# A quantised convolution and a spectral layer on one core: one row copy moves from VectorE to GpSimd, the per-image copies to ScalarE, and the per-image steps are spread out

## What is computed

```python
# layer 0: group norm, then a 3x3 convolution of int8-valued data, added to x
q  = clip(round(gn(x) * 127 / max|gn(x)|), -127, 127)
qw = clip(round(w * 127 / max|w|), -127, 127)
x  = x + conv3x3(q, qw) * (sx * sw / 127**2) + bias
# layer 1: group norm, then a mixing of 32 x 16 low frequencies, added to x
xf = rfft2(gn(x))[:, :, 32 rows, 16 columns]
x  = x + irfft2(einsum('ijab,ejab->eiab', R, xf))
```

## Time and profile before

| | us |
|---|---|
| median of three runs | 3821.65 |
| the profiled execution | 3827.99 |
| its span in the trace | 3826.2 |
| first stage, up to the first quantised tile | 786 |
| second stage, from the first quantised tile to the last | 786 to 2412 |
| per-image steps of the last image, mixing | 2430 to about 2550 |
| third stage | to the end |

### The profile page before, as it was taken

One profiled execution on the slowest core, in us unless ns is written; L12 is line 12 of the kernel. 1 busy time (PEld: TensorE's weight loads), 2 busy tenths in 40 slices (PEclk: granted clock), 3 DMA queues, 4 the chain that ended last, 5 costly groups with the idle time before them and its releaser, 6 DMA issues.

```text
span 3826.2 us, 82423 instructions
## 1 busy us (share of the span) xinstructions
PE 3155.1 (82%) x33434; PEld 1600.3 (42%) x33529; DVE 3273.9 (86%) x3398; ACT 2359.9 (62%) x3507; POOL 823.1 (22%) x1040
## 2 busy tenths in 40 slices
PE   5555556569999999999999999898888888888886
PEld 1111111146666666666666666673222222222222
DVE  6777888899999999989899999459888888888887
ACT  5777777758888887878788888433333333333332
POOL 0000000035455454545454544200000000000000
PEclk7777776689999999999999999759999999999998
DMA  9999999989999999999999999629999999999998
GB/s 366 358 360 357 360 367 359 343 240 355 336 316 341 309 352 298 354 299 349 302 348 323 327 336 316 198 96 424 427 427 427 427 427 427 427 425 421 421 421 372
DMA packets 342545, 1352.61 MB, mean 354 GB/s; under 512 B 45792, under 2 KB 47040, under 8 KB 243808
## 3 DMA queue, kind: packets, MB, share of 16 engines
q1 hardware_dynamic: 223104, 811.13, 58.9%
q0 software_dynamic: 82272, 268.58, 19.7%
q10 hardware_dynamic: 36864, 268.45, 16.7%
HBM read 811.10 MB, written 536.87 MB: 352 GB/s over the span
## 4 chain that ended last, share of the span: by engine, by line
DMA 41%; DVE 26%; PE 21%; ACT 5%; issue 4%; SPq 1%; POOL 1%; DVEq 0%; ACTq 0%
DMA out<-ring 18%; DMA ring<-in_x 12%; DVE ring L555 9%; DMA ring<-x_scratch 9%; PE ps L713 6%; DVE area L537 4%; ACT area L308 4%; PE ps L724 4%; PE ps L675 4%; DVE area L532 3%; DVE ring L650 2%; DVE area L541 2%; DMA x_scratch<-ring 2%; PE ps L734 2%; PE ps L816 1%
## 5 line engine op out<-in xcount | busy, mean ns | idle before, releaser
L284 POOL DMA_DIRECT2D x_scratch<-ring x1024 | 817.1, 805 | 1606.7 <-DVE ring L555 1583.9
L858 PE MATMUL ps<-x,gj_s 128*128 128x512 bf16 x2977 | 767.7, 407 | 221.2 <-DVE ring L650 213.8
L713 PE MATMUL ps<-area,wq 128*32 128x512 bf16 x12264 | 769.8, 385 | 58.0 <-DVE ring L555 32.8
L650 DVE TENSOR_TENSOR ring<-ps,ring 128x1024 f32<-128x1024 f32 x512 | 603.1, 1219 | 162.1 <-DMA ring<-x_scratch 158.7
L555 DVE SCALAR_TENSOR_TENSOR ring<-ps,sc,ring 128x1024 f32<-128x1024 f32 x512 | 634.6, 1278 | 22.4 <-PE ps L713 15.1
L675 PE MATMUL ps<-ring,negm_s 128*32 128x512 f32 x2048 | 387.4, 897 | 314.8 <-DMA ring<-in_x 314.8
L333 ACT ACTIVATE area<-ps 128x512 f32<-128x512 f32 x1024 | 553.4, 595 | 128.6 <-PE ps L724 127.5
L858 PEld LDWEIGHTS ps<-x,gj_s 128*128 128x128 bf16 x3072 | 295.0, 103 | 772.1 <-DVE ring L650 440.4
L724 PE MATMUL ps<-id_s,ring 128*128 128x128 f32 x4096 | 563.6, 281 | 17.8 <-ACT area L333 13.9
L461 DVE TENSOR_REDUCE stat<-area 128x1 f32<-128x4096 f32 x128 | 559.1, 4409 | 6.0 <-ACT area L308 5.8
L724 PEld LDWEIGHTS ps<-id_s,ring 128*128 128x128 f32 x4096 | 445.1, 142 | 169.3 <-issue 101.9
(11 more groups left out here) (123 smaller groups left out, 2158.9 us busy)
## 6 DMA issues: line engine op xcount, KB each, us to landing
ring<-in_x SPq DMA_DIRECT2D x256, 1024.0 KB, 7.8
ring<-in_x SPq DMA_DIRECT2D x1024, 256.0 KB, 6.7
x_scratch<-ring POOLq DMA_DIRECT2D x1024, 256.0 KB, 6.5
ring<-x_scratch SPq DMA_DIRECT2D x256, 1024.0 KB, 11.7
out<-ring ACTq DMA_DIRECT2D x256, 1024.0 KB, 25.3
ring<-in_rt SPq DMA_DIRECT2D x1, 4096.0 KB, 13.8
area<-in_gj SPq DMA_DIRECT2D x1, 768.0 KB, 4.5
eh_s<-in_eh SPq DMA_DIRECT2D x1, 128.0 KB, 2.1
```

Of the source, the lines that this page charges most:

```text
L284: pool.dma_start(x1_rows[b, m, r], xslot(t % SL)[32 * r:32 * r + 32, :].rearrange("p (g w) -> p g w", g=4)).then_inc(s_x_out[t % SL], 16)
L650: nc.vector.tensor_tensor(half, ps[0][:, hj * 2 * HW:(hj + 1) * 2 * HW], half, ALU.add).then_inc(s_add, 1)
L713: last = mm(ps[0][32 * cg:32 * cg + 32, HW * g:HW * g + HW], wq[:, (3 * a + dw) * C:(3 * a + dw + 1) * C], src[:, 1 + dw:1 + dw + HW], sta ...
L858: last = mm(bank(j), gj_s[:, (j * 3 + v) * 128:(j * 3 + v + 1) * 128], (z12, z12, z13)[v][:, k % 2], start=(v == 0), stop=(v == 2))
```

## The change

VectorE's lower-row copy (`q[64:128]` to `qs[0:64]`) goes to GpSimd, which makes it between its stores, with a semaphore of its own (`s_ql`) that the convolution waits for beside `s_q`. GpSimd's loop now runs over steps: in step i it stores tile i-3, then copies the rows of tile i. The eight `rows_copied` of each image go from VectorE to ScalarE. The later per-image steps are put at other j, and the loops run five steps longer, T + 20. In the diff `...` marks lines left out.

```diff
+        s_ql = sem("quantised_lower_rows_copied")
...
-            for t in range(T):
+            def lower_rows(t):
+                g0 = 4 * (t % 4)
+                pool.wait_ge(s_r, t + 1)
+                nc.gpsimd.tensor_copy(qs[0:64, g0:g0 + 4, :], q[64:128, g0:g0 + 4, :]).then_inc(s_ql, 1)
+
+            def store(t):
                 b, m = divmod(t, TB)
                 pool.wait_ge(s_ev, 2 * t + 2)
...
+            pool.wait_ge(s_qt, 1)
+            for i in range(T + 3):
+                if i >= 3:
+                    store(i - 3)
+                if i < T:
+                    lower_rows(i)
...  (scalar)
+            def rows_copied(b, n):
+                act.wait_ge(s_vt, 8 * b + n + 1)
+                act.activation(vt[:, :, 4 * n:4 * n + 4, :],
+                               bank(7).rearrange("p (c g k) -> p g c k", c=4, g=8), ACT.Copy).then_inc(s_vte, 1)
...
-                if small and j == 5:
+                if small and j == 6:
                     h_copied(b)
+                if small and 1 <= j < 5:
+                    rows_copied(b, 2 * j - 1)
                 if 4 <= i and i - 4 < T:
                     turned(i - 4, 0)
                     turned(i - 4, 1)
                     squared(i - 4)
+                if small and j < 4:
+                    rows_copied(b, 2 * j)
+                if 4 <= i and i - 4 < T:
                     turned(i - 4, 2)
                     turned(i - 4, 3)
-                if small and j == 8:
+                if small and j == 12:
                     root(b)
...  (vector)
-                nc.vector.tensor_copy(qs[0:64, g0:g0 + 4, :], q[64:128, g0:g0 + 4, :])
...
-                if small and 1 <= j < 5:
-                    rows_copied(b, 2 * j - 1)
...
-                if small and j < 4:
-                    rows_copied(b, 2 * j)
-                if small and j == 6:
+                if small and j == 8:
                     sums(b)
-                if small and j == 7:
+                if small and j == 11:
                     variance(b)
-                if small and j == 9:
+                if small and j == 14:
                     spectrum(b)
...  (tensor)
                 if h == 0:
                     pe.wait_ge(s_q, t + 2)
+                    pe.wait_ge(s_ql, t + 1)
...
-                if small and j == 6:
+                if small and j == 7:
                     dc_first(b)
-                if small and j == 7:
+                if small and j == 9:
                     spread(b)
-                if small and j == 9:
+                if small and j == 12:
                     spectra(b)
```

More of the change, by code:

```diff
@@ L361, in _ @@
             scaled(0)
-            for i in range(T + 15):
+            for i in range(T + 20):
                 b, j = divmod(i - (TB + 5), TB)
@@ L556, in combine @@
                                                op0=ALU.mult, op1=ALU.add).then_inc(s_ev, 1)
[L558 to L561, removed]
             def sums(b):
```

## The result

The change makes the kernel slower: 3857.09 us median (four runs, 3853.67 to 3862.18) against 3824.45 us for the kernel before on the same chip (3821.11 to 3829.39), a ratio of 1.0078 with a 95% interval of 1.006 to 1.0097. Run again beside the experiments it gave 1.0075 (1.0049 to 1.01). The prediction was 3765 us and faster.

What follows compares the result with a forecast made beforehand. VectorE was taken as the bound at 5.92 us a step, TensorE next at 5.75. From 3828.0 us, 55 for the images and 2 for the first 37 steps gave 3771 profiled, 3765 us median; range 3745 to 3835.

Steps and rivals of the forecast that it cites:

- What bounds the kernel: Second stage, plain steps: VectorE sets the pace at 5.92 us a step, TensorE's own pace is 5.75 us.
- VectorE's part: One copy of 0.72 us with its gap leaves each step, 5.92 to 5.20 us; waits of 5.0 us an image go.
- GpSimd's part: The new copy between stores takes 1.9 us and has 2.3 us of room under L555; GpSimd works 5.3 us a step.
- The rival on the other side: GpSimd's copy is slow and blocks VectorE; from about 2.7 us a net loss, about 3920 us at 3.5; chance 0.20.
- TensorE's part: As the next bound, TensorE takes 198.4 us an image instead of 206.5, a gain of 55 us over 6.81 images.
- ScalarE's part: The eight row copies an image moved to ScalarE cost nothing, 6.4 us a step against TensorE's 6.85.
- the late loads: ScalarE's waits for loads in the second stage: an allowance of 1.3 us an image.
- the time after the last tile: The per-image chain behind the last tile changes by zero, between -1 and +1 us.

Runs made afterwards that it cites:

- Experiment 1: The changed kernel with GpSimd's copy waiting for VectorE's last row copy of the tile instead of its rounding; 3804.69 us against 3831.47, ratio 0.9928.
- experiment 9: The changed kernel with GpSimd's copy replaced by a memset of the same 64x2064 elements at the same place; 4272.68 us in a single run.
- experiment 5: Kernel of Experiment 1 with the short per-image VectorE operations taking their second operand as a scalar from memory; 3786.14 us against 3826.52, ratio 0.9891.

## Why the prediction was wrong

- **What bounds the kernel** was right: VectorE at 5.92 us a step, TensorE behind it at 5.75. Experiment 1 puts plain steps at 5.76. A slip of the working, 37 x 0.19 where 5.92 - 5.75 gives 0.17, changes nothing, since 2 us were taken.
- **VectorE's part** was right in what it took away, 177 us of row copies and 44 us of `mixb` copies over the whole run, and wrong in that nothing came back. What came back is 174 us in the long pieces, 12 us in held scalings and 15 us in the root's multiplication. Its sum used the plain step of the earlier trace rows for all tiles. The tile in four with two pieces was in it as a few hundredths of a microsecond; it is the tile that decided.
- **GpSimd's part** is the step that failed. The copy's length was forecast as 1.9 us and measured as 1.92, its start 3.4 us behind the combining and measured as 1791.52 - 1788.15 = 3.4. The error was the sentence that it has "2.3 us of room, all of it under L555": I took the port as held from the copy's start to its end. For this copy it is taken once the copy has been let go and VectorE leaves it free, 0.96 us ahead of the start here, with two stores still ahead of the copy in GpSimd's order. In the tile with a seam between two copies that costs 2.7 us, 64 times. Of the two-input operations of the per-image work, which the prediction did not list among those that can be held, one an image is held in the changed kernel and two in experiment 1, for 2.2 us each.
- **The Trainium skill** (SBUF — State Buffer, "Who interferes with whom") says that a VectorE operation with two SBUF inputs contends with a GpSimd operation that reads SBUF and not with one that only writes. The runs agree on the copy, 2.37 us instead of 0.16 beside it. On a memset no run here shows it, since in experiment 9 these operations never ran beside one. I had weighed this section against L555 alone, where it says no and the trace says no (1.28 us after as before), and had not gone through the short operations with it.
- **The rival on the other side** named the right mechanism and the wrong condition: it asked for a copy of 2.7 us or more. A copy of 1.92 us was enough, through its early release. No term and no rival gave the release a price, and the result lies 22 us above the range.
- **TensorE's part** (198.4 us an image) was optimistic by about 2 us: with the holds of pieces and two-input operations gone, experiment 5 has images of 197 to 203, mean 200.5. The gain that the prediction put at 57 us is 40 us there.
- **ScalarE's part, the late loads and the time after the last tile** came out as said: ScalarE waits less for loads than before (49.6 us against 85.5), the added wait of TensorE on GpSimd's copy never shows, and the rest of the program behind the last tile is 1413 us against 1414.

## What to carry to other kernels

When a copy goes from VectorE to GpSimd, look at what VectorE does from the moment that the copy's wait is satisfied, not from the moment it would run: every seam between two of VectorE's fast copies and every operation with two SBUF inputs in that time can be held until GpSimd's operation ends. Let GpSimd's operation wait for the last of VectorE's operations that share the port, even if its data are ready earlier: here that moved one wait by 0.8 us and was worth about 1.5%. And cost a lighter engine on its rarest step too: a step that comes once in four or once in 32 has its own order and can undo the gain of the others.

## What the runs showed of the hardware

- A GpSimd copy of 64x2064 bf16 elements takes 1.92 us, a memset of them 1.84, a copy of 64x516 0.62 and of 64x4 0.20.
- A 64x1548 copy on VectorE takes 3.26 us instead of 0.55, and an operation on 128x1 elements with two SBUF inputs 2.37 instead of 0.16, when GpSimd's copy of 1.92 us has been let go ahead of them. The wait begins up to 0.96 us ahead of the copy's start in the trace.
- VectorE's scaling of 128x1024 float32 elements takes up to 2.28 us instead of 0.80 when GpSimd's copy is already running beside it.
- A GpSimd memset holds VectorE's copy behind the rounding that released it, 1.15 us ahead of its own start: 3.55 us instead of 0.69 for 64x2064 elements.
- GpSimd's descriptor work for four stores takes 3.31 us beside VectorE's copies, 2.89 beside a held one, and 2.18 alone; VectorE is not slowed by it (0.69 and 1.23 us throughout).
